# A four-part graph network: the first convolution turned into a slot layer, and an edge loop that only places and counts

## The reference, cut to what matters

```
h = relu(x @ proj.T + b)                         # part one: a gated graph network
for l in range(2):                               # two typed convolutions
    trans = einsum('nh,tdh->tnd', h, edge_W[l])  # one product per type
    agg   = segment_sum(trans[edge_type, src], dst)
    h     = relu(gru_cell(agg, h, ...))
x = layernorm(x + h @ out.T)
...                                              # part two: three relational convolutions,
                                                 #   each a mean by type and receiver, root and bias
...                                              # part three: one convolution against the edge direction, by degrees
...                                              # part four: node and edge attributes (16, mean over the edges)
                                                 #   into two dense layers
```

## Time and profile before

| | us |
|---|---|
| median of 3 runs | 2701.87 (2697.64 to 2702.93) |
| the profiled execution | 2686.08 |
| its span, first to last instruction | 2684.0 |
| TensorE busy | 2390.2 |
| VectorE busy | 1844.6 |
| GpSimd busy | 1591.1 |
| ScalarE busy | 856.3 |

### The profile page before, as it was taken

One profiled execution on the slowest core, in us unless ns is written; L12 is line 12 of the kernel. 1 busy time (PEld: TensorE's weight loads), 2 busy tenths in 40 slices (PEclk: granted clock), 3 DMA queues, 4 the chain that ended last, 5 costly groups with the idle time before them and its releaser, 6 DMA issues.

```text
span 2684.0 us, 45747 instructions
## 1 busy us (share of the span) xinstructions
PE 2390.2 (89%) x15645; PEld 2130.7 (79%) x15645; DVE 1844.6 (69%) x6137; ACT 856.3 (32%) x1498; POOL 1591.1 (59%) x1706
## 2 busy tenths in 40 slices
PE   7798888886877999879999989999899987987998
PEld 3587777773777998569999989999899985876896
DVE  4887777766775886687776588766567874443785
ACT  3476665652442111332222322212222210444002
POOL 0777777765566664755666367776377773677000
PEclk9899999998998999799999999999999997999999
DMA  8422222222997665179998799888899871677891
GB/s 299 125 65 63 61 63 62 63 51 92 252 253 212 181 172 147 32 225 280 281 276 257 249 294 287 260 265 253 276 282 271 261 203 39 213 261 240 262 268 55
DMA packets 271661, 520.15 MB, mean 194 GB/s; under 512 B 62015, under 2 KB 115698, under 8 KB 270645
## 3 DMA queue, kind: packets, MB, share of 16 engines
q1 hardware_dynamic: 185197, 289.49, 34.9%
q0 software_dynamic: 86224, 227.59, 29.3%
HBM read 323.93 MB, written 192.99 MB: 193 GB/s over the span
## 4 chain that ended last, share of the span: by engine, by line
PE 50%; POOL 20%; DMA 12%; issue 8%; DVE 7%; ACT 2%; DVEq 0%; SPq 0%; POOLq 0%; ACTq 0%
PE ps L984 21%; POOL msg L694 15%; PE ps L956 9%; PE ps L969 6%; PE ps L1199 5%; DMA rec<-chunks,idx 4%; DMA chunks<-xs 3%; DMA chunks<-xo,put_idx 2%; POOL chunks L792 2%; POOL rec L694 2%; DVE shot L1902 1%; PE ps L1174 1%; POOL attributes L703 1%; PE ps L1018 1%; DMA srow<-lanes_of_slots 1%
## 5 line engine op out<-in xcount | busy, mean ns | idle before, releaser
L694 POOL DMA_INDIRECT rec<-chunks,idx x596 | 589.4, 989 | 366.8 <-PE ps L984 142.6
L984 PE MATMUL ps<-dhot,rec 128*128 128x168 f32 x4768 | 739.4, 310 | 52.2 <-DMA rec<-chunks,idx 29.7
L984 PEld LDWEIGHTS ps<-dhot,rec 128*128 128x128 f32 x4768 | 694.8, 192 | 71.1 <-DVE dhot L1923 37.3
L1923 DVE TENSOR_SCALAR dhot<-iota,dcode 128x168 f32<-128x168 f32 x2384 | 589.1, 311 | 93.7 <-PE ps L984 85.5
L956 PE MATMUL ps<-hrow,shot 126*128 126x128 f32 x4000 | 498.7, 279 | 51.5 <-DVE shot L1902 39.6
L956 PEld LDWEIGHTS ps<-hrow,shot 126*128 126x128 f32 x4000 | 477.9, 194 | 64.0 <-issue 32.4
L694 POOL DMA_INDIRECT msg<-messages,idx_buf x416 | 400.0, 962 | 195.7 <-issue 195.4
L1302 ACT ACTIVATE xs<-ps 128x512 f32<-128x512 f32 x500 | 296.8, 597 | 668.4 <-PE ps L956 604.9
L703 POOL DMA_INDIRECT attributes<-w,rank_to x368 | 373.9, 1016 | 178.9 <-issue 119.1
L1902 DVE TENSOR_SCALAR shot<-srow,lane_no 126x512 f32<-126x512 uint8 x500 | 232.3, 490 | 89.7 <-DMA srow<-lanes_of_slots 50.1
L848 PE MATMUL ps<-big,lane1h 128*128 128x300 f32 x832 | 224.0, 423 | 0.7 <-ACT big L1285 0.7
(11 more groups left out here) (289 smaller groups left out, 2495.6 us busy)
## 6 DMA issues: line engine op xcount, KB each, us to landing
chunks<-xs SPq DMA_DIRECT2D x375, 256.0 KB
tmp<-inverse_counts SPq DMA_DIRECT2D x36, 1008.0 KB, 10.3
chunks<-xs SPq DMA_DIRECT2D x125, 258.0 KB
srow<-lanes_of_slots SPq DMA_DIRECT2D x100, 320.0 KB, 5.7
grec<-chunks SPq DMA_DIRECT2D x125, 256.0 KB
messages<-big SPq DMA_DIRECT2D x25, 504.0 KB
trow<-lanes_of_targets SPq DMA_DIRECT2D x30, 320.0 KB, 4.1
rec<-chunks,idx POOLq DMA_INDIRECT x596, 5.0
```

Source lines behind the costliest of these rows:

```text
L694: eng.indirect_dma_start(buf, None, table, bass.IndirectOffsetOnAxis(ap=index, axis=0)).then_inc(sem, 16)
L984: last = mm(ps[:, 4 + i % 2, (v % 3) * WT:(v % 3 + 1) * WT], rec[:, v % RS, j * P:(j + 1) * P], dhot[:, v % DS, j * WT:(j + 1) * WT], star ...
L1923: last = vec.tensor_scalar(dhot[:, v % DS, j * WT:(j + 1) * WT], iota[:, 0:WT], dcode[:, v, j:j + 1], None, ALU.is_equal)
```

## The change

The message table goes, and with it the gathers and the message sum of the edge loop; the loop still places slots and counts. The first convolution becomes slot layer 1, all tiles ahead of all windows, with the codes (now copied by ScalarE). The second convolution becomes layer 2, whose tiles and windows are woven as `plan` says, by itself. The relational layers are 3 to 5. So there are five slot layers in place of four.

Attributes: GpSimd now computes the rows of every second group inside the loop (`rows_of_ranks`, nine operations on 128x8) and sends them from the loop's own `mark` buffers (`send_marks`, eight transfers). A buffer is loaded again only when its sends have landed (`marks_sent`). The other 26 groups are sent as 128 tiles from one load beside layer 1's tiles, and 80 beside layer 2's windows.

At the start the index data are loaded ahead of features and weights. VectorE no longer copies `state` products for the first GRU (ScalarE does), and the first GRU stands between layers 1 and 2.

```diff
-AT = {1: range(0, 12), 2: range(12, 28), 3: range(28, 39), 4: range(39, 50), 5: range(50, 52)}
-AT_FIRST = {1: 32, 2: 80, 3: 40, 4: 40}
+LATE_GROUPS = NG // 2
+AT = {1: range(0, 16), 2: range(16, LATE_GROUPS)}
+AT_FIRST = {1: 16, 2: 6}
...
+        def woven(k):
+
+            for kind, n in plan(k):
+                yield kind, n
+                if kind == "sums" and n % GW == 4 and n >= GW:
+                    yield "transform", n // GW - 1
+            yield "transform", NGRP - 1
...
-            table_stores(0, flat)
             eng.wait_ge(q("zeros"), 1)
...
-            for it in range(PASSES):
-                for s in range(SUB):
-                    eng.wait_ge(q("attr_kept"), it * SUB + s + 1)
-                    eng.dma_start(mark[:, s, :], mark_d[:, ds((it * SUB + s) * (G * TC), G * TC)])\
-                       .then_inc(q(f"mark_loaded_{s}"), 16)
+            for g in range(NG):
+                eng.wait_ge(q("attr_kept"), g + 1)
+                if g % 2 == 0 and g >= SUB:
+                    marks_sent(eng, g - SUB)
+                eng.dma_start(mark[:, g % SUB, :], mark_d[:, ds(g * (G * TC), G * TC)])\
+                   .then_inc(q(f"mark_loaded_{g % SUB}"), 16)
...
+            def rows_of_ranks(g):
+
+                tiles = slice(g * G, (g + 1) * G)
+                eng.wait_ge(q("slot_known"), g + 1)
+                st.did(eng.tensor_scalar(sent[:, 0, :], rank_f[:, tiles], float(CAP), 1e6, ALU.is_ge, ALU.mult))
+                st.did(eng.tensor_scalar(sent[:, 1, :], src_sb[:, tiles], float(CAP), None, ALU.mult))
+                st.settle()
+                st.do(eng.tensor_tensor(sent[:, 1, :], sent[:, 1, :], sent[:, 0, :], ALU.add))
...
+                st.do(eng.tensor_copy(rank_to[:, tiles], sent[:, 1, :]))
...
-            for it in range(PASSES):
-                for s in range(SUB):
-                    eng.wait_ge(q("idx_staged"), it * SUB + s + 1)
-                    eng.sem_inc(q("rows_known"), 1)
-                    for t in range(G):
-                        rows_of(msg[:, s, t, :], table_rows, idx_buf[:, s, t:t + 1], q(f"gathered_{s}"))
...
+            rows_of_ranks(0)
+            for g in range(0, NG, 2):
+                if g + 2 < NG:
+                    rows_of_ranks(g + 2)
+                send_marks(g)
             eng.wait_ge(q("code_ready"), 1)
-            eng.wait_ge(q("rows_cleared"), 32)
-            for n in range(AT_FIRST[1]):
+            for n in range(G * len(AT[1])):
                 send_attrs(1, n)
...
+                    if k == 2 and v == 0:
+                        for n in range(AT_FIRST[2]):
+                            send_attrs(2, n)
+                    if k == 2 and v % 2 == 1 and AT_FIRST[2] + v // 2 < G * len(AT[2]):
+                        send_attrs(2, AT_FIRST[2] + v // 2)
...
-                    for t in range(G):
-                        last = mm(ps[:, g % 2, 0:P], msg[:, g % SUB, t, :], onehot[:, g % 2, t, :], start=t == 0,
-                                  stop=t == G - 1)
-                    last.then_inc(q("summed"), 1)
...
+            first_layer()
             for i in range(NCH + 1):
                 if i < NCH:
                     gru(0, i)
...
             after(eng, "gru_cand", 0, NCH)
             candidate_state(1)
-            first_layer()
+            second_layer()
...
+                    if k == 1:
+                        act(xs[:, i % XS, 4 * P:RECORD_COLS], code[:, 4 * i:4 * i + 4], ACT.Copy)
```

More of the change, by code:

```diff
@@ new lines, in first_layer, with second_layer @@
+            def first_layer():
+                for i in range(NQ):
+                    store_tile(1, i)
+                eng.wait_ge(q("inv_ready"), INV_PIECES)
+                eng.dma_start(inv_d, acc[TYPE_ROWS, 0:NU]).then_inc(q("inv_stored"), 16)
+                after(eng, "acc_evac", 1, NGRP)
+                general(1)
+                for s in range(NS - 1):
+                    lanes_load(2, s)
+                after(eng, "gru_h", 0, NCH)
+                attr_load(2)
+            def second_layer():
+                for kind, i in woven(2):
+                    if kind == "tile":
+                        store_tile(2, i)
+                after(eng, "acc_evac", 2, NGRP)
+                general(2)
+                for s in range(NS - 1):
+                    lanes_load(3, s)
@@ L998, in first_layer, with second_layer @@
                 general(1)
+            def second_layer():
+                for kind, n in woven(2):
+                    if kind == "tile":
+                        spread_slots(2, n)
+                    elif kind == "sums":
+                        sum_window(2, n)
+                    else:
+                        transform(2, n)
+                after(eng, "acc_evac", 2, NGRP)
+                general(2)
             def other_layers():
@@ L1060, in _ @@
             eng.wait_ge(q("loop_done"), 1)
+            for c in range(NCH):
+                turn_rows(1, c)
+            eng.wait_ge(q("src1_ready"), 1)
+            for j in range(4):
+                last = mm(ps[0:NQ, 7, j * P:(j + 1) * P], src1[:, j * NQ:(j + 1) * NQ], wt("ident"), start=True, stop=True)
+            last.then_inc(q("lanes_mm"), 1)
+            eng.wait_ge(q("lanes_ready"), 1)
+            eng.wait_ge(q("cells_known"), 1)
+            mm(ps[0:TB, 7, 0:NWP], wb("before", TB, TB), cells, start=True, stop=True).then_inc(q("starts_mm"), 1)
+            first_layer()
             for i in range(NCH + 1):
@@ L1328, in layer @@
                     eng.wait_ge(q("bad_known"), 1)
+                elif k == 2:
+                    for kind, n in woven(2):
+                        if kind == "tile":
+                            keep_tile(2, n)
+                        elif kind == "transform":
+                            keep_sums(2, n)
+                        else:
+                            if n % 3 == 2 and n >= 5:
+                                keep_three(2, n // 3 - 1)
+                            if n == NW - 1:
+                                for i in range((NW - 3) // 3, NTRI):
+                                    keep_three(2, i)
                 else:
@@ L1941, in layer @@
                     return
+                if k == 2:
+                    for kind, n in woven(2):
+                        if kind == "tile":
+                            slot_hot(2, n)
+                        elif kind == "sums":
+                            type_hot(2, n)
+                    after(eng, "acc_evac", 2, NGRP)
+                    general(2)
+                    return
                 for kind, j, n in joined():
@@ L2059, in _ @@
                    .then_inc(q("res_used"), 1)
-            layer(2)
+            layer(3)
             degrees()
```

490 lines of the change are left out of this document (205 added, 285 removed).

## The result

The changed kernel takes 2894.18 us (median of 4 runs, 2882.1 to 2901.92) where the kernel before takes 2701.94 in the same session: ratio 1.0711, 95% interval 1.0672 to 1.075, slower. 2907 was predicted, with a range of 2860 to 2965. The profiled execution of the changed kernel is the longest of the four, 2901.92 us with a span of 2900.1; the one of before was a short one. A second session on another chip gave 2881.51 in 4 runs, ratio 1.0679 [1.0644, 1.0713], and a profile with a span of 2869.8 at the clock of before (0.963 against 0.964). Sizes are judged by that one, and this is why both stand here.

What follows compares the result with a forecast made beforehand. GpSimd's gathers were taken to bound the old edge loop, TensorE the stages from 838 us on. Terms summed to +205 on a profiled 2686.1 (2891); with 15.8 for the median, 2907 us, range 2860 to 2965.

Steps and rivals of the forecast that it cites:

- Start: Before the edge loop: table copies go and index loads come first, so the loop starts at 50.5 us, not 97.0 (-46).
- Loop: Edge loop: without gathers and message sum, 51 passes of 7.8 us plus 10.5, 510 to 408 us (-102).
- the ring: Edge loop: a mark buffer is reused only after its group's sends land; 31 us over four passes, 7.8 each.
- Loop end to first tile: Between edge loop and first tile: the GRU moves away, slot and cell lists stay exposed, 67 to 17.5 us (-49.5).
- Tiles: First slot layer's tile stage: lists and attributes add transfers, 128 sends end at 175 to 184; 164 to 184 us (+20).
- GRU: First GRU, now on its own behind the first slot layer: +59 us.
- Second layer: Second convolution as woven slot layer: 327 us of TensorE plus waits for transfers, sends and hiccups, +352 us.
- Later layers: Last two slot layers: 176 sends leave them, 14 us less a layer, -28 us; bounds 10 and 40 in all.
- Forecast as summed: Whole kernel: the terms hold as added up, own range 2880 to 2935 us; chance 0.63.
- rival of a held-up GpSimd: Edge loop: small operations wait for VectorE, +2.7 us in the ring or up to twice that, 2943 to 2977; chance 0.17.
- everything hides: Loop at VectorE's 7.5 us a pass, extra bytes fit, layer two at 345: about 2868 us; chance 0.17.
- rival on the other side: Whole kernel gets faster, for which the loop would have to run at 3.9 us a pass; chance 0.02.

Runs made afterwards that it cites:

- control run: The changed kernel, unchanged, run again in the second session on another chip: 2881.51 us, ratio 1.0679 to the kernel before.
- a3: Changed kernel with GpSimd's nine small operations done twice for each second group, four mark buffers kept: 3174.04 us, 8.76 us a pass.
- a4: Changed kernel with eight mark buffers and GpSimd's nine small operations done twice: 3124.14 us, 7.76 us a pass.
- a1: Changed kernel with eight mark buffers in place of four: 3128.5 us, ratio 1.0249 to the kernel before on that chip, 8.05 us a pass.
- d1: Changed kernel with eight mark buffers, run once more in the third session: 3114.56 us, ratio 1.0228, 7.88 us a pass.
- d2: Changed kernel with eight mark buffers and the 208 late sends in three parts in place of two: 3058.09 us, ratio 1.0067 to the kernel before.
- b1: Changed kernel with 64 attribute sends in place of 128 in the first slot layer's tile stage: 2862.43 us.
- b2: Changed kernel with 26 of the second layer's 80 sends ahead of its first gather: 2869.27 us, ratio 1.0643.
- d3: Kernel before with four of the eight message gathers a pass left out: 2843.46 us, against 3033.46 whole on the same chip.
- a2: Changed kernel with the loop's attribute sends and all waits on them taken out, the nine operations kept: 3086.63 us, 7.46 us a pass.

## Why the prediction was right, and where it was not

The medians of the result differ by 192 us and those of the second session by 181, where 205 was forecast. The forecast added 15.8 us to the profiled time because the profile of before was that much under its median; the profiled execution of the result was the longest of four. The one number of 2907 therefore hit more closely than its parts did.

Each step, with its size in the control run:

- **Start, -46.** 48.4 and 49.6 against 50.5. Right.
- **Loop, 408.** 407.6, and 417.4 in the first profile. Size and mechanism are right. The small operations cost what I took (3.3 for 3.1), the ring carries GpSimd's work (a3 against a4), and VectorE's pass without a wait is 7.54 us with the ring 0.24 above it. What the runs do not show is the other half of the proof, that the pass falls to 7.5 when the ring opens: all three runs of it (a1, d1, d2) fell on delayed chips and lost 0.2 to 0.5 us a pass to late signals, and whether eight buffers have a part in these was not tried. By the control's waits the gain would be 12 us at most, an estimate (0.24 x 51).
- **Loop end to first tile, 17.5.** 17.2.
- **Tiles, 184.** 184.8, but this hit is luck. By my terms the sends end at 175 and the transfers at 184; in fact the sends are the later end, at 184.8, and the transfers would end at 172.6 (b1). The sends began 2.3 us after the first tile, as taken, but lasted 176.5 us in place of 164 (1.38 each). The transfers gave less than their bytes: the tiles took 162.9 us against 153.0 before (first matmul to last), 10 more where the bytes alone would have given 21. "Both ways end together" was wrong by 12 us.
- **Windows, 229; GRU, +59.** 229.2; 56.6.
- **Second layer, +352.** 355.8. The sum of TensorE's work (327) stands against 334.8 busy, 8 more. Of the 15 for the six sends and hiccups, b2 gave back 9 as idle time.
- **Later layers, -28.** This term is mis-sized: -40. The stage from the third layer's first tile to the last window takes 1032.7 us where 1073.0 stood before, and TensorE's idle time in it fell from 56 to 27 us. I took 14 for each of the last two layers and nothing for the one before. By the starts of the layers they gave 2.5, 13 and 25. The last had the most to gain because there TensorE waited longest for gathered chunks, 15.8 us in 14 waits; in the control these are 2.5 us in one. Only 29 of the 40 us are idle time; TensorE's busy time fell by 11 at the same number of products, and why is open. The -40 lies at the edge of the bounds of 10 and 40. The stage behind the layers moved by -5 and +10 in the two profiles; that is no effect of the change.

The sum by the control's trace: -48.6 - 102.4 - 49.8 + 20.8 + 0.2 + 56.6 + 355.8 - 1.3 - 40.3 - 5.2 = +185.8, and 2869.8 - 2684.0 is 185.8. The prediction's +205 is 19 above it, of which 12 are the later layers and 5 a stage that the change leaves alone. The first session's profiled run has +216 in its place. "Forecast as summed" with its own range of 2880 to 2935 held. The rival of a held-up GpSimd did not come at its size: it wanted 2.7 us for nine operations, and VectorE adds some 0.7 (next paragraph). Nor did "everything hides": the sends showed at the end of the tile stage, and the loop stayed at 7.8. The rival on the other side is answered by the same stages: the most that a run of the second session took off was 13 us in the second layer and 12 in the tile stage, against 186.

The one rule cited, from the Trainium skill, page "SBUF — State Buffer", section "Who interferes with whom", has conditions that the prediction left out; one is a VectorE instruction with two inputs in SBUF beside a GpSimd instruction that reads SBUF. The trace agrees for such a pair: the last of the nine operations, the cast, starts in all 19 groups of the control (150 to 450 us) while VectorE's scan of two inputs runs. It ends with the scan and takes 0.52 us, where most casts in a4, started elsewhere, take 0.19 (last section). The other eight take 0.20 to 0.37 us. Against the shortest of each in a3 and a4 the nine are some 0.7 us longer in all. So the rule shows plainly in one operation of nine, and the price of 0.35 came near to it by two errors: an operation takes 0.29 us in the mean where 0.19 was read, and the step to the next 0.08 where 0.15 was assumed.

## What to carry to other kernels

Moving work from the engine that is full in one stage to the engine that is full in all the others can shorten that stage and lose in sum: here the loop gave back 102 us and the two stretches beside it 98, and another layer and a bare GRU cost 412. Cost such a change by stage, on the engine that ends last in each, and price the displaced cover (the GRU under which lists and attributes used to arrive) like work of its own. And ask of each stage what stands close behind its bound: the old loop had TensorE 1.5 us a pass behind GpSimd, and the new one has VectorE 0.24 us behind the ring, so the removal of the first alone gives less than its own rows promise. A third point is for the reading of experiments: a rerun on another chip can bring waits of its own, so look at what ended the waits before a time is taken as an answer.

## What the runs showed of the hardware

**On some chips signals between engines come late while GpSimd sends.** In a1 GpSimd sends 128 tiles of attributes between 498.7 and 664.9 us. The tile stage up to then, and after it (columns as in the earlier trace rows):

```profile
496.30:665.00 168.70, 31.22 (x160) 28.50 (x160) 12.79 (x22) 11.75 (x34) 123.47 (x128) 0.54 0.21 65
665.00:819.10 154.10, 107.01 (x842) 102.02 (x842) 94.79 (x178) 72.95 (x216) 3.73 (x4) 0.89 0.80 231
```

20 tiles pass TensorE beside the sends, and the other 105 in 143 us behind them. The transfers do not fill this time: their share is 0.21 beside the sends. The engines wait for each other. The longest waits between 500 and 660 us, and one of them from both sides:

```profile
DVE shot L1900 <- remote: 134.1, 7, 22.0
ACT xs L1293 <- remote: 130.4, 7, 21.8
```

```profile
539.94 2.07 PE L958 MATMUL ps<-hrow,shot 126*128 126x128 f32 x8 [14.13 <-ACT xs L1294]
561.64 0.20 ACT L1293 ACTIVATE xs<-code 128x4 f32<-128x4 f32 x1 [21.75 <-remote]
```

Line 958 is the tile product, line 1293 ScalarE's first copy for that tile. TensorE is through at 542.0, and ScalarE, idle all the while, starts its copy 19.6 us later. SyncE can store only what ScalarE has copied, three stores in 45 us. The tile stage takes 323 us in place of 185. It is so in every run of the changed kernel on these chips (323 to 334 us, and 264 in d2, which sends 80 tiles there). The kernel before stands there too, if not in its first tile stage (160.7 us in d3), where its sends alternate with copies. Its largest group of such waits, over the whole of d3:

```profile
ACT xs L1302 <- remote: 265.4, 95, 11.1
```

No profile of the result or of the second session has one such wait. GpSimd keeps its pace, 1.30 us a send in a1. Where it sends nothing in the loop (a2), none falls between 150 and 450 us. What sets the delay off is not known, nor whether it makes up all of the 330 to 340 us that the kernel before loses on these chips.

**GpSimd and VectorE hold up each other's small instructions.** The casts between 150 and 450 us, in the control and in a4 (ns: shortest, median, longest), and one of the control with the scan beside it:

```profile
L730 POOL CAST rank_to<-sent x19: 517/518/522, 163.2 to 440.0; 128x8 int32<-128x8 f32 x19
L732 POOL CAST rank_to<-sent x37: 189/190/531, 152.7 to 449.4; 128x8 int32<-128x8 f32 x37
```

```profile
178.16 0.63 DVE L1548 TENSOR_TENSOR_SCAN sb_seen<-sb_go,sb1h 128x225 f32<-128x225 f32 x1
178.25 0.52 POOL L730 CAST rank_to<-sent 128x8 int32<-128x8 f32 x1
```

The scan began first and ends at 178.79, the cast at 178.77; so it is, to 0.02 us, in all 19. In a4 the steps have moved against each other, and one cast meets the scan.

The other way round it is VectorE that waits. Its copy of 25 columns between 150 and 450 us, in the control, and without sends (a2):

```profile
L1544 DVE COPY sb1h<-sb_seen 128x25 f32<-128x25 f32 x38 | 11.4, 299 | 0.0
```

```profile
L1537 DVE COPY sb1h<-sb_seen 128x25 f32<-128x25 f32 x37 | 6.7, 182 | 0.0
```

The mean hides three cases. 17 of the 38 copies in the control start 0.57 to 0.59 us behind the start of a send, end with it and take 0.39 us. 19 start just behind one of the nine small operations and take 0.23. Two meet neither and take 0.17. Copies that start at other moments of a send are not longer (0.18 in a3 and a4), which is why the means there are 215 and 254 ns. At 0.12 us a pass it decides nothing here.
